# Moving weight loads of layer 0's experts behind its attention, and the order of the filling of layer 1

## The chip, the cores and the metric

The kernel runs on one core of a Trainium2 chip. The core has TensorE (PE, matrix products), VectorE (DVE), ScalarE (ACT), GpSimd (POOL) and SyncE (SP), which here only issues DMAs. Each engine runs its own program in order and waits on semaphores that others raise. The metric is the time of one execution on the device, in microseconds.

## What is computed

Two layers on 64 sequences of 64 positions and 256 channels, all in float32. Each layer is a cross attention and a mixture of experts, each with a residual:

```python
x = x + xattn0(layernorm(x), ctx)       # rotary, 8 heads of 8, projection
x = x + ffn0(layernorm(x))              # 64 experts, top 8, no capacity
x = x + xattn1(layernorm(x), ctx)       # 8 heads of 8
x = x + ffn1(layernorm(x))              # 64 experts, top 8, capacity 128 rows for each expert

def moe(x, router, gate, up, down):     # 4096 tokens
    topw, topi = top_k(softmax(x @ router), 8)
    topw = topw / topw.sum(-1)
    for each chosen expert e:  y += topw_e * (silu(x @ gate[e]) * (x @ up[e])) @ down[e]
```

An expert's weights are gate and up (128 x 384 floats, 192 KB) and down (96 x 256 floats, 96 KB).

## The kernel before

**Attention of a layer** is a software pipeline over 32 pairs of sequences. Step `s0` of it works on pair `s0 - LAG[stage]` at each stage: load 0, comb 1, front 2, stack 3, smax 4, attn 5, back 6, route 7, place 8, post 9. `steps` calls `body` on each engine for 41 steps, and most engines cut a step into 16 units `u`. Buffers are three deep (`NB`).

- *front*: the normalised rows `xn` are projected to q and k (`qk`, L1523). ScalarE, GpSimd and ScalarE again split them into three bf16 parts: `parts[0]` (L954), `rem` (GpSimd L779), `parts[1]` (ACT L963), and GpSimd's third part (L787).
- *stack*: SP writes the parts to DRAM (`q_stack_d`, `k_stack_d`, L621) and reads them back as stacked operands `q2`, `k2` (L645).
- *smax*: 16 score tiles `psS` (PE L1479), whose row maxima DVE takes (`mx`, L1086). The maxima of each half are turned (`mT0`), cut to bf16 (`mhi`, ACT) and a remainder (`mlo`, DVE `split_max`), and SP puts both into `q2` (L655).
- *attn*: the scores again, less the maxima, ScalarE's Exp into `prob` (L886), products with `v`.
- *route, place, post*: the router, the eight chosen experts, the row of each. In layer 0 GpSimd scatters every normalised row to its eight places in `xs_d` (L728).
- *comb*, layer 1 only: a step fetches the eight results of a pair with GpSimd's gathers `yg` (L741), four are scaled by ScalarE (`ys`, L893, `s_comb`), four are scaled and added by DVE (`add_row`, L1130, `s_sum`), which makes `x2` and its moments (`sums`). GpSimd's `roots` make the scale of the layer norm of it, ScalarE `xn`. SP stores `x2` to `x2_d` (L660); it is read again at attn. A gather waits until the buffer of the pair before has been used.

The first steps of layer 1, up to `FULL` = 6, have no full load for the units and an order of their own: `units_of_sum` and `units_of_products` place the sums and the products, and `sums` of pair 2 stand in step 4 after eight maxima.

**Experts of layer 0** are 320 tiles of 128 rows, sorted by expert. `slots` is a pipeline with one tile in each slot: gather by SP 4 slots behind, transposes (X) 8, gate and up products (GU) 9, transposition of the hidden tile (H) 10, down product (D) 11. ScalarE copies the transposed tile (`xgT`, L984), takes Silu (L989) and copies the result (`y_all`, L993). PE waits at every eighth slot for the weights of the next eight experts (`d_w`).

**Weights** go into `wt`, which shares SBUF with the attention's tiles and fills it from the top. Room for `EARLY` = 12 experts is left free by the attention, and ScalarE issues their loads in steps 9 to 14. The other 52 are issued by ScalarE, expert `s0 + 12` at the head of slot `s0`, so that nine loads stand before its first copy of a tile. Between the attention and the slots of a layer stands a barrier of all five engines; in layer 0 DVE makes a table of the tiles ahead of it, SP clears the end of the lists (`clear_end`) and reads the table, and GpSimd waits for its scatters.

What sets the order is the code itself: each engine's program is written out in the order in which it runs.

## Time and profile before

| | |
|---|---|
| median of 3 runs | 2065.82 us (2065.47 to 2069.38) |
| the profiled execution | 2065.41 us, of which the span of the trace is 2063.7 us |
| layer 0's attention | 0 to 605 us, scatters and table until the barrier opens at 647 |
| layer 0's experts | 647 to 1123 us |
| layer 1's attention | 1126 to 1798 us, its last routing until 1820 |
| layer 1's experts | 1820 to 2063 us |
| busy over the span | PE 81%, PE weight loads 55%, DVE 68%, ACT 61%, POOL 48% |

The slices of the page, each 51.6 us, show PE at 9 nearly everywhere but for two dips, around 625 us and around 1150 us, and the end. DMA-issuing instructions are not counted as busy, so an engine that issues loads looks idle in the profile and is not.

### The profile page before, as it was taken

The numbers are of one execution on the slowest core, as the hardware profiler recorded it, in microseconds if no ns is written. First come the engines' busy times: TensorE is split into PE (matmuls) and PEld (weight loads), VectorE is DVE, ScalarE is ACT, GpSimd is POOL, SyncE is SP. The second block draws the span as 40 slices with busy tenths as digits, with TensorE's granted clock in tenths as the row PEclk, the third lists the DMA queues.
The fourth block names the chain that finished last, engine by engine and source line by source line (L and its number), as shares of the span: only waits on it lengthen the run. The fifth ranks groups of instructions, "written<-read, shape, count | busy, mean of one in ns | idle before, by whom it ended". The sixth has DMA issues, their size and how long they took to land. (4 is left out here: it accounts for less than half of the span.)

```text
span 2063.7 us, 45000 instructions
## 1 busy us (share of the span) xinstructions
PE 1665.0 (81%) x12724; PEld 1130.1 (55%) x12879; DVE 1412.1 (68%) x4335; ACT 1264.0 (61%) x3300; POOL 985.5 (48%) x1114
## 2 busy tenths in 40 slices
PE   3999999999973999999997268888888888845651
PEld 1555555555543789888986134444444444444530
DVE  5888888888854455545434469999999999743330
ACT  1777677777761566666665258888888887621210
POOL 4367677777763000000001666666666663148883
PEclk9999999999995999999999589999999999969896
DMA  5678877777736966666665578898778876178856
GB/s 139 160 210 243 224 213 213 210 211 216 202 119 185 346 213 202 198 198 201 196 199 160 138 187 202 227 233 199 194 195 200 195 195 151 51 187 186 177 93 111
DMA packets 413088, 390.98 MB, mean 189 GB/s; under 512 B 46640, under 2 KB 385072, under 8 KB 412848
## 3 DMA queue, kind: packets, MB, share of 16 engines
q1 hardware_dynamic: 341888, 259.97, 47.3%
q0 software_dynamic: 37904, 90.22, 17.6%
q10 hardware_dynamic: 33056, 37.90, 6.2%
q8 instruction: 113, 1.85, 0.4%
q14 instruction: 127, 1.04, 0.2%
HBM read 233.74 MB, written 170.16 MB: 196 GB/s over the span
## 5 line engine op out<-in xcount | busy, mean ns | idle before, releaser
L1086 DVE TENSOR_REDUCE mx<-psS 128x2 f32<-128x512 f32 x1024 | 678.9, 674 | 112.3 <-PE psS L1479 72.5
L886 ACT ACTIVATE prob<-psE 128x512 f32<-128x512 f32 x1024 | 601.1, 595 | 227.6 <-PE psE L1492 211.6
L741 POOL DMA_INDIRECT yg<-y_d,row_all x256 | 249.7, 975 | 642.7 <-SPq L401 484.1
L1492 PE MATMUL psE<-q,k 128*128 128x256 bf16 x2048 | 395.2, 275 | 38.8 <-ACT prob L886 16.1
L1479 PE MATMUL psS<-k,q 128*128 128x512 bf16 x869 | 337.0, 390 | 32.8 <-DMA k<-k_stack_d 26.2
L1602 PE MATMUL psE<-wt,xgT 128*128 (+1 forms) x1536 | 325.8, 336 | 6.1 <-ACT xgT L984 5.6
L1431 DVE TENSOR_TENSOR hid<-sil,psE 128x96 f32<-128x96 f32 x384 | 97.6, 254 | 333.0 <-ACT sil L989 332.8
L728 POOL DMA_INDIRECT xs_d<-xr,row_all x256 | 252.6, 987 | 109.3 <-ACT prob L886 65.4
L1492 PEld LDWEIGHTS psE<-q,k 128*128 128x128 bf16 x2048 | 186.0, 98 | 194.3 <-ACT prob L886 70.6
L1508 PE MATMUL psO<-prob,v 128*32 128x256 f32 x4096 | 275.9, 387 | 8.5 <-ACT osb L866 8.5
L984 ACT COPY xgT<-psS 128x256 f32<-128x256 f32 x384 | 144.5, 376 | 197.4 <-PE psS L1596 137.5
L1602 PEld LDWEIGHTS psE<-wt,xgT 128*128 128x128 f32 x1536 | 247.9, 195 | 12.2 <-issue 10.8
L1596 PE MATMUL psS<-ident,xg 128*128 128x128 f32 x768 | 154.7, 284 | 100.5 <-DMA xg<-xn_d,idx 84.9
L1614 PE MATMUL psM<-wt,hT 96*128 (+1 forms) x768 | 233.1, 385 | 0.0
L1596 PEld LDWEIGHTS psS<-ident,xg 128*128 128x128 f32 x768 | 105.1, 144 | 159.7 <-DMA xg<-xn_d,idx 82.3
L1479 PEld LDWEIGHTS psS<-k,q 128*128 128x128 bf16 x1024 | 103.9, 102 | 153.2 <-issue 71.5
L993 ACT COPY y_all<-psM 128x256 f32<-128x256 f32 x320 | 119.2, 373 | 86.6 <-PE psM L1614 86.2
L1508 PEld LDWEIGHTS psO<-prob,v 128*32 128x32 f32 x4096 | 109.8, 109 | 104.1 <-issue 49.2
L989 ACT ACTIVATE sil<-psE 128x96 f32<-128x96 f32 x384 | 96.7, 252 | 88.2 <-PE psE L1602 87.6
L1614 PEld LDWEIGHTS psM<-wt,hT 96*128 96x128 f32 x768 | 118.1, 194 | 15.2 <-issue 0.4
L1523 PE MATMUL psM<-xn,proj_q 128*128 128x256 f32 x126 | 44.4, 436 | 74.0 <-ACT xn L930 37.5
L787 POOL TENSOR_TENSOR parts<-rem,parts 128x512 bf16<-128x512 f32 x64 | 74.9, 1171 | 50.3 <-ACT parts L963 49.4
(219 smaller groups left out, 2632.4 us busy)
## 6 DMA issues: line engine op xcount, KB each, us to landing
xg<-xs_d SPq DMA_DIRECT2D x320, 128.0 KB, 2.6
y_d<-y_all SPq DMA_DIRECT2D x320, 128.0 KB, 2.3
q<-q_stack_d SPq DMA_DIRECT2D x128, 256.0 KB
k<-k_stack_d SPq DMA_DIRECT2D x128, 256.0 KB
wt<-in_gu ACTq DMA_DIRECT2D x128, 192.0 KB, 3.7
q_stack_d<-parts SPq DMA_DIRECT2D x64, 192.0 KB
k_stack_d<-parts SPq DMA_DIRECT2D x64, 192.0 KB
wt<-in_dn ACTq DMA_DIRECT2D x128, 96.0 KB, 4.2
```

The lines of the kernel that those rows point to most:

```text
L728: g.indirect_dma_start(xs_d[:, :], bass.IndirectOffsetOnAxis(row_all[:, row(st.pair(stage) * K + k, 1)], 0), xr[b][:, 0:T], None).then_inc ...
L741: g.indirect_dma_start(yg[:, k, :], None, y0_d[:, :], bass.IndirectOffsetOnAxis(row_all[:, row(st.pair("load") * K + k, 1)], 0))\
L886: a.activation(prob[gr][:, u % 4, :], psE[ring][:, :], ACT.Exp, scale=SCALE).then_inc(s_exp, 1)
L984: a.copy(xgT[st.buf("X", 2)][:, :, :].rearrange("p c t -> p (c t)"), psS[st.buf("X", 2)][:, 0:2 * P]).then_inc(s_xgT, 1)
L993: a.copy(y[st.buf("D")], psM[st.buf("D", 2)][:, 0:T]).then_inc(s_y, 1)
L1086: v_.tensor_reduce(mx[b][:, bg // 4, :].rearrange("p (h r) -> p h r", h=2)[:, :, (bg % 4) * 2 + tt], psS[(UNITS * (st.s0 - LAG["smax"]) + ...
L1479: m_.matmul(psS[(UNITS * (st.s0 - LAG["smax"]) + u) % 3][:, :], q2[b][:, bg, tt * P:(tt + 1) * P], k2[b][:, bg, :], start=True, stop=True) ...
L1492: ins = m_.matmul(psE[ring][:, i * T:(i + 1) * T], k2[b][:, bg, hh * T + i * P:hh * T + (i + 1) * P], q2[b][:, bg, :], start=True, stop=True)
L1508: ins = m_.matmul(psO[32 * j:32 * j + 32, (q % 2) * T:(q % 2 + 1) * T], v[b][:, i, 4 * q + j, :], prob[gr][:, j, i * T:(i + 1) * T], start ...
L1596: ins = m_.transpose(psS[i][:, c * P:(c + 1) * P], xg[b][:, c * P:(c + 1) * P], ident[:, :])
L1602: ins = m_.matmul(psE[i][:, 0:2 * I], xgT[i][:, c, :], weights_of(st, "GU", table, P, 2 * I * c, 2 * I), start=(c == 0), stop=(c == 1))
L1614: m_.matmul(psM[i][:, 0:T], hT[i][:, :], weights_of(st, "D", table, I, 4 * I, T), start=True, stop=True).then_inc(s_yp, 1)
```

## The change

- The tiles `q2`, `k2` and `prob` are allocated last in the attention, so that, once they are no longer used, room for `FIRST` = 30 experts lies free at the top of SBUF.
- After the last step with a back stage in layer 0, SP waits for the last maxima, exponentials and products, and then issues experts 12 to 21, and after the last step experts 22 to 29 (`load_soon`). With nothing between them on SP, these are 18 experts in a row.
- ScalarE issues the other 34 in layer 0's slots, starting at slot 8, two in every three slots. In layer 1 nothing changes in this.
- ScalarE executes a Silu of one column ahead of the barrier in both layers, which loads the table for it.
- In layer 1 SP stores `x2` of a pair one step later, behind the reading of the stack and ahead of the maxima (before: behind the maxima and at once).
- In step 5 of layer 1 GpSimd does the first four gathers, then the remainder and the third part, then the other four.
- In step 4 of layer 1 DVE does `split_max` after eight maxima and ahead of pair 2's sums, not after eleven.

```diff
+SOON, LATER = 10, 8
+FIRST = EARLY + SOON + LATER
...
+        def load_soon(sp, first, n):
+            sp.wait_ge(s_max, UNITS * PAIRS)
+            sp.wait_ge(s_exp, UNITS * PAIRS)
+            sp.wait_ge(s_pv, 4 * PAIRS)
+            for e in range(first, first + n):
+                load_weights(sp, 0, e)
...
@@ block.sync, body
+                summed = Step(1, st.s0 - 1)
+                if L == 1 and summed.on("comb"):
+                    b, t = summed.buf("comb"), summed.pair("comb")
+                    hold(sp, s_x2, summed.n1("comb"))
+                    sp.dma_start(x2_d[row(t), :], x2[b][:, :]).then_inc(d_x2[b], 16)
                 if L == 0 and 0 <= st.s0 - CLEAR_AT < PAIRS:
...
-                if st.on("comb") and L == 1:
-                    b, t = st.buf("comb"), st.pair("comb")
-                    hold(sp, s_x2, st.n1("comb"))
-                    sp.dma_start(x2_d[row(t), :], x2[b][:, :]).then_inc(d_x2[b], 16)
                 if st.on("back"):
...
+                if L == 0 and st.s0 == LAG["back"] + PAIRS - 1:
+                    load_soon(sp, EARLY, SOON)
 
             for L in range(2):
                 steps(L, body)
+                if L == 0:
+                    load_soon(sp, EARLY + SOON, LATER)
...
@@ block.gpsimd, body, layer 1
-                    if st.s0 >= FULL - 1:
+                    if st.s0 >= FULL:
                         for k in range(K):
                             gather(st, k, PACE[L][k])
+                    elif st.s0 == FULL - 1:
+                        for k in range(4):
+                            gather(st, k, 0)
                     remainder()
                     third_part()
                     if st.s0 < FULL - 1:
                         for k in range(AHEAD_OF_ROOTS):
+                            gather(st, k, 0)
+                    elif st.s0 == FULL - 1:
+                        for k in range(4, K):
                             gather(st, k, 0)
...
@@ block.scalar
             def slot_body(st, table):
-                if st.s0 < E - EARLY:
-                    load_weights(act, st.L, st.s0 + EARLY)
+                for e in range((FIRST, EARLY)[st.L], E):
+                    if st.s0 == (FLAG["X"] + (e - FIRST) * 3 // 2, e - EARLY)[st.L]:
+                        load_weights(act, st.L, e)
...
             for L in range(2):
                 steps(L, body)
+                act.wait_ge((s_wk, s_wall)[L], PAIRS)
+                a.activation(ex[:, 0:1], ex[:, 0:1], ACT.Silu)
                 barrier(act, 2 + 2 * L)
...
@@ block.vector, body
+                filled = L == 1 and st.s0 == FULL - 2
...
-                    if u == 10 and st.on("smax"):
+                    if u == 10 and st.on("smax") and not filled:
                         split_max("smax", 0)
...
-                    if L == 1 and st.s0 < FULL - 2 - 1 and u == 15:
-                        sums(st, 0)
-                    if L == 1 and st.s0 == FULL - 2 and u == 7:
+                    if filled and u == 7:
+                        split_max("smax", 0)
                         sums(Step(1, FULL - 3), 0)
-                    if L == 1 and st.s0 == FULL - 2 and u == 15:
+                    if L == 1 and st.s0 < FULL - 1 and st.s0 != FULL - 3 and u == 15:
                         sums(st, 0)
```

ScalarE at the start of layer 0's slots. Before, behind the last router's exponential (`ex`), stand nine pairs of loads, here the end of them, and then the first tile:

```order
L522 DMA wt<-in_dn 96x256
L521 DMA wt<-in_gu 128x384
L522 DMA wt<-in_dn 96x256
L521 DMA wt<-in_gu 128x384
L522 DMA wt<-in_dn 96x256
L984 COPY xgT<-psS 128x256
L521 DMA wt<-in_gu 128x384
L522 DMA wt<-in_dn 96x256
L984 COPY xgT<-psS 128x256
L989 ACT_TABLE_LOAD
L989 ACTIVATE sil<-psE 128x96
```

The same place of the changed kernel, from the last exponential on:

```order
L999 ACTIVATE ex<-top,ntop 128x8
L1024 ACT_TABLE_LOAD
L1024 ACTIVATE ex<-ex 128x1
L526 DMA wt<-in_gu 128x384
L527 DMA wt<-in_dn 96x256
L1010 COPY xgT<-psS 128x256
L526 DMA wt<-in_gu 128x384
L527 DMA wt<-in_dn 96x256
L1010 COPY xgT<-psS 128x256
L1015 ACTIVATE sil<-psE 128x96
```

One pair of loads is left ahead of the first copy, and the table load stands ahead of the barrier.

SP in steps 3 and 4 of layer 1. Before, from the reading of pair 0's stack (`q_0`, `k_0`), the store of pair 2's x2 (`x_d<-x_2`) stands ahead of pair 1's stack:

```order
L645 DMA q_0<-q_stack_d 64x2048
L645 DMA k_0<-k_stack_d 64x8x256
L660 DMA x_d<-x_2 128x256
L570 DMA xin<-x_d 128x256
L621 DMA q_stack_d<-parts 128x3x256
L621 DMA q_stack_d<-parts 128x2x256
L621 DMA q_stack_d<-parts 128x256
```

The same place of the changed kernel:

```order
L659 DMA q_0<-q_stack_d 64x2048
L659 DMA k_0<-k_stack_d 64x8x256
L666 DMA x_d<-x_1 128x256
L584 DMA xin<-x_d 128x256
L635 DMA q_stack_d<-parts 128x3x256
L635 DMA q_stack_d<-parts 128x2x256
L635 DMA q_stack_d<-parts 128x256
```

In the place of pair 2's store now stands pair 1's, a step older; pair 2's stands behind the reading of pair 1's stack.

GpSimd in step 5 of layer 1. Before, with three gathers left over from step 4 in the 11:

```order
L759 TENSOR_TENSOR rstd<-below,rstd 128x2
L741 DMA yg<-y_d,row_all 128x256 x11
L779 TENSOR_TENSOR rem<-qk,parts 128x512
L787 TENSOR_TENSOR parts<-rem,parts 128x2x256
L754 TENSOR_SCALAR ve<-mv 128x2
```

The same place of the changed kernel:

```order
L778 TENSOR_TENSOR rstd<-below,rstd 128x2
L760 DMA yg<-y_d,row_all 128x256 x7
L798 TENSOR_TENSOR rem<-qk,parts 128x512
L806 TENSOR_TENSOR parts<-rem,parts 128x2x256
L760 DMA yg<-y_d,row_all 128x256 x4
L773 TENSOR_SCALAR ve<-mv 128x2
```

Four gathers moved from ahead of the remainder to behind the third part.

## Rows read from the trace of the kernel before

**Rows 1.** Timeline, first dip: start us, us, engine, line, operation, count, [idle before <-releaser].

```profile
610.49 0.33 SPq L664 DMA_DIRECT2D x_d<-x  x1
...
640.88 0.96 POOL L728 DMA_INDIRECT xs_d<-xr,row_all  x1 [0.30 <-issue]
...
647.37 0.33 ACTq L521 DMA_DIRECT2D wt<-in_gu  x1
...
650.84 1.17 PE L1596 MATMUL psS<-ident,xg 128*128 128x128 f32 x4 [14.74 <-DMA xg<-xs_d]
...
655.93 0.37 ACT L984 COPY xgT<-psS 128x256 f32<-128x256 f32 x1 [34.09 <-issue]
...
657.33 1.28 ACT L989 ACT_TABLE_LOAD   x1
```

**Rows 2.** Windows: busy us (instructions) by engine, PEclk, DMA share, GB/s; scatters.

```profile
605.00:642.00 37.00, 9.60 (x55) 5.52 (x45) 16.74 (x80) 3.82 (x10) 28.50 (x33) 0.61 0.29 101
```

**Rows 3.** Windows of layer 0's expert products, with and without weight loads.

```profile
662.00:727.00 65.00, 63.35 (x366) 52.26 (x365) 29.47 (x112) 35.96 (x122) 0.00 (x0) 1.00 1.07 344
737.00:1037.00 300.00, 300.00 (x1902) 269.67 (x1902) 149.85 (x572) 189.81 (x634) 0.00 (x0) 1.00 0.66 199
```

**Rows 4.** Timeline of ScalarE, one slot with a load.

```profile
668.17 0.37 ACT L993 COPY y_all<-psM 128x256 f32<-128x256 f32 x1 [0.18 <-PE psM L1614]
...
669.09 0.37 ACT L984 COPY xgT<-psS 128x256 f32<-128x256 f32 x1 [0.55 <-PE psE L1602]
...
669.67 0.37 ACT L993 COPY y_all<-psM 128x256 f32<-128x256 f32 x1
```

**Rows 5.** Timeline of SP's queue in the filling of layer 1.

```profile
1154.74 1.51 SPq L621 DMA_DIRECT2D q_stack_d<-parts  x3
...
1179.85 0.33 SPq L660 DMA_DIRECT2D x_d<-x  x1
...
1180.75 1.46 SPq L621 DMA_DIRECT2D q_stack_d<-parts  x3
```

**Rows 6.** Timeline of the other engines in the filling of layer 1.

```profile
1149.83 1.44 POOL L787 TENSOR_TENSOR parts<-rem,parts 128x512 bf16<-128x512 f32 x1 [0.73 <-ACT parts L963]
...
1164.86 1.15 POOL L787 TENSOR_TENSOR parts<-rem,parts 128x512 bf16<-128x512 f32 x1 [0.73 <-ACT parts L963]
...
1170.49 1.68 PE L1479 MATMUL psS<-k,q 128*128 128x512 bf16 x3 [9.40 <-DMA k<-k_stack_d]
...
1176.57 0.48 DVE L1130 SCALAR_TENSOR_TENSOR ys<-yg,w_all,xin 128x256 f32<-128x256 f32 x1
...
1177.02 0.26 ACT L873 CAST mhi<-psM 16x128 bf16<-16x128 f32 x1 [2.21 <-PE psM L1521]
...
1188.11 0.48 DVE L1130 SCALAR_TENSOR_TENSOR ys<-yg,w_all,xin 128x256 f32<-128x256 f32 x1 [2.56 <-DMA yg<-y_d,row_all]
...
1192.72 0.18 DVE L1168 BATCH_NORM_AGGREGATE mv<-stats 128x2 f32<-128x6 f32 x1
...
1194.89 0.69 DVE L1086 TENSOR_REDUCE mx<-psS 128x2 f32<-128x512 f32 x1 [1.99 <-PE psS L1479]
...
1195.88 0.24 POOL L754 TENSOR_SCALAR ve<-mv 128x2 f32<-128x2 f32 x1
...
1197.67 1.07 POOL L741 DMA_INDIRECT yg<-y_d,row_all  x1 [0.16 <-issue]
...
1206.53 0.95 POOL L741 DMA_INDIRECT yg<-y_d,row_all  x1 [5.26 <-ACT ys L893]
...
1217.81 0.62 ACT L963 CAST parts<-rem 128x512 bf16<-128x512 f32 x1 [6.76 <-POOL rem L779]
...
1234.86 1.16 POOL L779 TENSOR_TENSOR rem<-qk,parts 128x512 f32<-128x512 f32 x1
```

**Rows 7.** Timeline of ScalarE at the end of layer 1's attention.

```profile
1817.53 0.72 ACT L903 ACTIVATE hote<-hote,part 128x512 bf16<-128x512 bf16 x1 [3.40 <-DVE hote L1205]
...
1819.96 0.33 ACTq L521 DMA_DIRECT2D wt<-in_gu  x1
```

More of the change, by code:

```diff
@@ L284, in build @@
         parts = [ab(f"parts{b}", [P, 2, 3, T], BF16) for b in range(NB)]
-        q2 = [ab(f"q2_{b}", [P, 8, T], BF16) for b in range(NB)]
-        k2 = [ab(f"k2_{b}", [P, 8, 2 * T], BF16) for b in range(NB)]
         mx = [ab(f"mx{b}", [P, 2, 16]) for b in range(NB)]
@@ L290, in build @@
         v = [ab(f"v{b}", [P, 2, UNITS, 32]) for b in range(NB)]
-        prob = [ab(f"prob{g}", [P, 4, 512]) for g in range(3)]
         osb = ab("osb", [P, GROUPS, T])
@@ L321, in build @@
         zf = xr[0]
-        assert nc.sbuf_bytes_remaining >= 4 * EARLY * WIDTH
+        below_these = nc.sbuf_bytes_remaining
+        q2 = [ab(f"q2_{b}", [P, 8, T], BF16) for b in range(NB)]
+        k2 = [ab(f"k2_{b}", [P, 8, 2 * T], BF16) for b in range(NB)]
+        prob = [ab(f"prob{g}", [P, 4, 512]) for g in range(3)]
+        assert nc.sbuf_bytes_remaining >= 4 * EARLY * WIDTH and below_these >= 4 * FIRST * WIDTH
         att.close()
```

## The prediction

> **What bounds the kernel now.** I read the slices of the page first: layer 0's attention, a dip near 625 us, the expert products of layer 0 up to 1123 us, a second dip, layer 1's attention, its products. The change touches the two dips and the first 50 slots of the products of layer 0, so I opened the timeline at both dips and the windows by stage.
>
> First dip [rows 1]. The last attention output is stored at 610.49, but GpSimd goes on scattering rows, one each 1.26 us (0.96 busy, 0.30 idle), until 641.8. The barrier opens at 647.4. GpSimd bounds this stretch; the DMA engines are 0.29 busy [rows 2]. Then TensorE has the first tile transposed from 650.84, but ScalarE copies it only at 655.93: it was issuing the weights of nine experts, 18 DMAs. Five microseconds of a waiting TensorE are ScalarE's queue.
>
> Layer 0's products. Nine multiplies are one tile. While weights are loaded, 366 of them take 65 us, so 40.7 tiles at 1.60 us; afterwards 1902 take 300 us, 211.3 tiles at 1.42 us [rows 3]. ScalarE's loop shows why that can be: with a load a slot lasts 1.50 us, 0.55 us of it a gap for the issue [rows 4]. But the DMA share is 1.07 there, 0.66 later [rows 3], so two limits coincide.
>
> Second dip [rows 5, 6]. Here the filling of layer 1's pipeline waits on one queue, SP's. The third bf16 part of pair 0 is ready at 1151.27 (1149.83 + 1.44), its stack goes out at 1154.74. Pair 1's is ready at 1166.02 and goes out at 1180.75, right behind the store of pair 2's x2 at 1179.85, which SP had to wait for. TensorE's first scores, after 9.40 us idle, and step 5's wait for those stacks. Later ScalarE is idle 6.76 us for GpSimd's remainder of pair 3, which stands behind eight gathers.
>
> **The change, part by part.**
>
> 1. Weights of experts 12 to 29 on SP from 610.9. SP issues 36 DMAs; at ScalarE's rate (18 in the 8.56 us from 647.37 to 655.93, 0.48 each) they take 17 us, until 628. Moved behind them on SP: the clearing of the end of the lists and the reading of the table, for which SP waits until DVE has it; the barrier needs GpSimd's scatters to land anyway, 19 us after 628, so the 17 us on SP cost nothing. What of DMA capacity? In the loading window a tile without loads would take 0.66 x 1.42 = 0.94 us of all engines; it takes 1.07 x 1.60 = 1.71, so an expert costs 0.77 us. A scatter costs 0.29 x 37 / 27 = 0.40 us (33 instructions of GpSimd, six of them roots) [rows 2, 3]. From 611 to 642: 18 x 0.77 + 25 x 0.40 = 23.9 us in 31, and in the 17 us of issue 19.4 against 18.2 at a share of 1.07: a backlog of about 1 us, gone by 632. I take zero for the barrier; between a gain, which nothing on this path could give, and a delay, if scatters run at half rate for those 17 us, 14 x 1.26 = up to 17 us. Near zero is the row's own value, since the sum fits.
>
> The Trainium skill (DMA: Bandwidth & Descriptors, Issuing engines are not separate DMA queues) says that DMAs of all engines run on the same 16 engines and interleave, so that another issuer saves issue time only. By it the 18 experts are no cheaper on SP than on ScalarE and the sum for the barrier stands or falls with the capacity above; ScalarE's issue time is what is saved, as items 2 and 3 have it. No row before shows scatters beside SP loads.
>
> 2. ScalarE's head start. The 16 DMAs of slots 0 to 7 are gone; slot 8 issues one pair before the tile arrives. The copy can follow the transposes by 0.65 us: 651.5 instead of 655.93, **4.4 us**; between 3.9 and, if the tile lands earlier without the weights beside it, 5.4.
>
> 3. The pace. 34 experts are left, at two per three slots, up to slot 57. Two slots of 1.50 and one of 0.95 (1.50 less the gap of 0.55) are 1.32 us of ScalarE per slot, under TensorE's 1.42. The DMA demand becomes 0.66 + 34 x 0.77 / 71 = 1.03, just under 1.07. The excess was 65 - 40.7 x 1.42 = 7.2 us. If each load kept its price, 34/40.7 of it would remain: a gain of 1.2. If none did, 7.2. I take **5.8**, nearer the second because both limits are then undershot, one barely.
>
> 4. The Silu table. Its load of 1.28 us [rows 1] leaves layer 0's first slots, where TensorE ran on beside it: 0.2 us, between 0 and 0.5. In layer 1 it stands between the copy for the lists (ends 1818.25) and the barrier, past which ScalarE issues at 1819.96 [rows 7]: 1.28 and a one-column Silu just fit. Zero, between -0.4 and +0.3.
>
> The Trainium skill (ScalarE: Activation LUTs, What ACT_TABLE_LOAD costs) puts a drain of about 1.38 us behind each such load. Estimated by that page, layer 1's barrier would come about 1 us later and the total would be 1 us higher; the row before has 1.28 and shows no drain, which speaks against it here.
>
> 5. The fill. I move each event by what released it. Pair 0's stack: 1154.74 becomes 1151.3, so -3.4, and the first scores (1170.49) come at 1167.1. In step 4 VectorE now waits for the split of the maxima ahead of the sums: the bf16 maxima end at 1177.28 and the subtraction at 1177.55, against sums that started at 1176.57, +1.0. So pair 2's sums, the last gathers of pair 3 that wait for them, and pair 3's sums move by -2.4. VectorE ended those at 1192.90 and then waited until 1194.89 for the stack; now the stack is there first (its store moves by up to 14.7; the context load behind it on SP waits for pair 0's V product, still 10 us ahead of before) and step 5 starts at 1190.5, -4.4. Three score tiles are ready by then, which saves perhaps 0.6 more: pair 5's first gather moves from 1206.53 to 1201.5. Then the remainder stands behind four gathers, not eight: 1201.5 + 4 x 1.26 = 1206.5, done 1207.6, where ScalarE had it at 1217.81: -10.2. That is not kept. GpSimd now is the chain: the remainder and third part to 1209.6, four gathers to 1214.7, the roots (1.8, from 1195.88 to 1197.67), eight gathers to 1226.6, and the remainder of step 6 starts there instead of 1234.86: **8.2 us**. By then GpSimd has caught up (8 x 1.26 + 3.1 + 1.8 = 15 us of work in a step of 18). Below, if the sums or the products ahead of the gathers refuse to move with the stack, it is 3; above, if GpSimd's gathers in step 6 overlap better than drawn, 10.5.
>
> 6. In all later steps of layer 1 SP stores x2 one step later, between the stack's loads and the maxima. It waits for nothing there, and VectorE carries these steps. Zero; between -3 and +5 over 27 steps, since a DMA ahead of the maxima could cost 0.2 a step.
>
> Sum: 4.4 + 5.8 + 0.2 + 0 + 8.2 = 18.6. The profiled execution took 2065.4, of which the span is 2063.7; that is 0.4 below the median 2065.8. So 2046.8 on its scale, **2047** on the median's.
>
> **The rivals.**
>
> A. The fill gives 3 only, since VectorE's sums of pair 3 wait for gathers, which wait for sums (the 2.0 us behind 1192.90 is all the stack itself held). For it: at 1188.11 pair 3's sums start after 2.56 us of waiting for a gather; against: GpSimd's gathers demonstrably stand ahead of the remainder. 2047 + 5.2 = 2052.
>
> B. In the products the DMA engines, not ScalarE, are the limit, and at 1.03 they still are: 1.2 instead of 5.8, 2052. Against: demand falls by a third.
>
> C. The weights slow the scatters. Each later scatter waits for its turn: half rate for half of the 17 us gives 8.5 back, 2056.
>
> D. Slower than before: the same place as C, but GpSimd's issue itself stalls while SP's descriptors fill the engines, and the whole row of about 25 scatters stretches. It decides from 18.6 / 25 = 0.74 us more per scatter (1.26 to 2.0); at 1.0 more the time is 2072. Against: the demand of that stretch fits, as item 1 has it.
>
> E. It doesn't do what it says: the barrier moves by as much as the products gain and the fill only shifts waits; within 4 us of before.
>
> F. Parts 3 and 5 at their upper ends: 2042.
>
> The Trainium skill (DMA: Bandwidth & Descriptors, Queues, rings and completion order) says that each DMA engine takes turns between the queues that have work. By this rule the scatters' queue keeps its turn and C and D would not occur; no row of before tests it, so they keep their chances.
>
> **How the numbers follow.** Forecast 0.50, A 0.16, B 0.12, C 0.07, D 0.04, E 0.03, F 0.08. The forecast's own spread is 2043 to 2051. The upper bounds of items 2, 3 and 5 together give 2042, the lower ones 2058 (3.9 + 1.2 + 3 = 8.1). A range of 2040 to 2058 leaves out D, E, and half of F: about 0.15 with the tails. A measurement of this kernel tells 0.2%, 4 us, from no change. Faster by more: all but D, E, 0.93; within 0.2%: 0.03; slower: 0.04.
>
> **What would show it.** Right: SP issues 36 weight DMAs between 611 and 629 and the barrier stays at 647.4; first copy of a tile at 651.5; tiles at 1.42 to 1.48 us from the start; counted from layer 1's first gather, pair 0's stack 3.4 us, pair 1's 11 to 15, step 5's first maximum 4 and the remainder of step 6 8 us earlier than before. Wrong: a barrier past 650; tiles still at 1.55 with ScalarE's gaps gone (B); step 5 moved but the remainder of step 6 not (A); steps of layer 1 longer than before by more than 0.2 us.

## The result, and the profile after

Timed in turn with the kernel before, the changed kernel took 2050.23 us in the median (2047.69 to 2055.02, 4 runs) against 2066.34: a ratio of 0.9922, 95% interval 0.9906 to 0.9939. Timed again in another series it had 2051.67 us, 0.9938 (0.9926 to 0.9951). It is 13 to 16 us faster where 18.8 were forecast; 2047 was 3 to 5 us too low, within the range of 2040 to 2058.

The profiled execution of after took 2055.02 us, its span is 2053.3, 10.4 below before. Cut at events that both traces have (the last scatter; the first transposed tile's copy; the first, 71st and last of ScalarE's 320 copies of a tile's product; layer 1's first gather and its first transposed tile's copy), that span divides like this, in us:

| stretch | before | after | gain | forecast |
|---|---|---|---|---|
| start to the last scatter | 640.88 | 641.82 | -0.9 | 0 |
| last scatter to the first transposed tile's copy | 15.05 | 10.72 | 4.3 | 4.4 |
| from there to the first product's copy | 6.1 | 6.1 | 0 | 0.2 |
| 70 tiles, while weights are loaded | 107.6 | 107.6 | 0.0 | 5.8 |
| the other 249 tiles | 353.1 | 354.6 | -1.5 | 0 |
| last product's copy to layer 1's first gather | 3.2 | 2.5 | 0.7 | 0 |
| layer 1's attention, to its first tile's copy | 702.6 | 694.6 | 8.0 | 8.2 |
| layer 1's experts | 235.2 | 235.2 | 0.0 | 0 |

Two terms of the sum are there, within 0.2 us each, and one is missing in this pair of traces. Two rows vary too much to be read: the 249 tiles without loads took 352.5 to 355.4 us in the kernels below that leave them alone, and the last scatter stands at 637.9 to 643.8 us in the other traces of kernels that took 2049 to 2059 us (641.5 in fill_only, which has no loads on SyncE there). This profiled execution is also the slowest of its four, so its 10.4 us is less than the 16.1 us between the medians; which stretch was quicker in the others no trace shows. The first dip first, in the timeline of after (start us, us, engine, line, operation, count, [idle before <- releaser]); it answers to [rows 1]:

```profile
612.10 0.33 SPq L679 DMA_DIRECT2D x_d<-x  x1
612.54 0.38 SPq L526 DMA_DIRECT2D wt<-in_gu  x1
...
622.80 1.28 ACT L1024 ACT_TABLE_LOAD   x1
...
641.82 0.96 POOL L747 DMA_INDIRECT xs_d<-xr,row_all  x1 [0.30 <-issue]
...
648.33 0.33 ACTq L526 DMA_DIRECT2D wt<-in_gu  x1
...
652.54 0.37 ACT L1010 COPY xgT<-psS 128x256 f32<-128x256 f32 x1 [27.92 <-PE psS L1624]
```

SyncE issues weights from 612.54, and GpSimd's last scatter still is 0.96 us with 0.30 us of idle time ahead. The barrier opens 6.5 us behind that scatter, as before. ScalarE has one pair of loads left ahead of its first copy, at 652.54, which waits for the transposes and no longer for ScalarE's own issues.

The windows (stretch, then busy us and instructions of PE, PE weight loads, DVE, ACT, POOL; PEclk, DMA share, GB/s), against [rows 2] and [rows 3]:

```profile
605.00:642.00 37.00, 11.06 (x59) 6.76 (x59) 17.31 (x84) 5.72 (x14) 28.43 (x36) 0.61 0.77 244
662.00:727.00 65.00, 62.50 (x367) 51.94 (x366) 29.46 (x111) 36.00 (x123) 0.00 (x0) 1.00 0.94 288
```

In the first dip the DMA engines went from a share of 0.29 to 0.77 and GpSimd did as much as before. In the second line is the surprise: with a third fewer loads (27 experts in these 65 us, before 40) and a DMA share of 0.94 instead of 1.07, 65 us hold 367 multiplies, before 366.

The filling of layer 1, against [rows 5] and [rows 6]; layer 1's first gather is at 1123.49 here, at 1125.94 before:

```profile
1148.76 1.45 SPq L635 DMA_DIRECT2D q_stack_d<-parts  x3
...
1157.72 0.62 SPq L666 DMA_DIRECT2D x_d<-x  x1
...
1163.49 1.43 SPq L635 DMA_DIRECT2D q_stack_d<-parts  x3
```

```profile
1164.24 2.49 DVE L1114 TENSOR_REDUCE mx<-psS 128x2 f32<-128x512 f32 x4 [12.19 <-remote]
...
1182.26 0.48 DVE L1158 SCALAR_TENSOR_TENSOR ys<-yg,w_all,xin 128x256 f32<-128x256 f32 x1 [2.54 <-DMA yg<-y_d,row_all]
...
1186.98 1.86 DVE L1114 TENSOR_REDUCE mx<-psS 128x2 f32<-128x512 f32 x3
...
1203.39 1.17 POOL L798 TENSOR_TENSOR rem<-qk,parts 128x512 f32<-128x512 f32 x1
...
1223.97 1.16 POOL L798 TENSOR_TENSOR rem<-qk,parts 128x512 f32<-128x512 f32 x1
```

Counted from the first gather, pair 0's stack goes out 25.27 us later (28.80 before), pair 1's 40.00 (54.81), since no store stands ahead of it that waits. Pair 3's sums start at 58.77 (62.17), still after 2.54 us of waiting for a gather. Step 5's first maximum starts right behind them at 63.49 (68.95), without the wait for the stack, and the remainder of step 6, 1223.97 - 1123.49 = 100.48, was at 108.92.

### The profile page after: what moved, and what is told of

Read it like the earlier page. It is cut to its first block and busy times, and to the rows that moved or that the text cites. A ratio compares the mean times of both kernels' runs of the same rounds, so it can differ in the third digit from the quotient of the medians.

```text
span 2053.3 us, 45004 instructions
## 1 busy us (share of the span) xinstructions
PE 1665.0 (81%) x12724; PEld 1127.2 (55%) x12879; DVE 1414.6 (69%) x4335; ACT 1265.1 (62%) x3302; POOL 983.7 (48%) x1114
## 5 line engine op out<-in xcount | busy, mean ns | idle before, releaser
L760 POOL DMA_INDIRECT yg<-y_d,row_all x256 | 248.7, 971 | 632.2 <-SPq L406 480.7
L1507 PE MATMUL psS<-k,q 128*128 128x512 bf16 x869 | 336.5, 389 | 22.4 <-DMA k<-k_stack_d 12.8
L1624 PEld LDWEIGHTS psS<-ident,xg 128*128 128x128 f32 x768 | 103.7, 143 | 165.2 <-DMA xg<-xn_d,idx 90.7
L806 POOL TENSOR_TENSOR parts<-rem,parts 128x512 bf16<-128x512 f32 x64 | 74.8, 1169 | 50.4 <-ACT parts L988 49.5
```

The source lines that it names most:

```text
L760: g.indirect_dma_start(yg[:, k, :], None, y0_d[:, :], bass.IndirectOffsetOnAxis(row_all[:, row(st.pair("load") * K + k, 1)], 0))\
L1507: m_.matmul(psS[(UNITS * (st.s0 - LAG["smax"]) + u) % 3][:, :], q2[b][:, bg, tt * P:(tt + 1) * P], k2[b][:, bg, :], start=True, stop=True) ...
L1624: ins = m_.transpose(psS[i][:, c * P:(c + 1) * P], xg[b][:, c * P:(c + 1) * P], ident[:, :])
```

## Where the missing term went

For each kernel I took the starts of ScalarE's copies of tile products (y_all from psM). The time from one start to the next is called a slot below. An undisturbed tile takes 1.415 us. The last columns count the slow slots and give what they have over 1.415 us each. The first 54 tiles, in us:

| kernel | first, 55th copy at | 54 tiles | over 54 x 1.415 | slots of 1.45 to 1.9: number, excess | slots over 1.9 |
|---|---|---|---|---|---|
| before | 662.00, 746.87 | 84.9 | 8.5 | 27, 6.6 | 3, 1.8 |
| after | 658.71, 743.64 | 84.9 | 8.5 | 25, 5.9 | 3, 2.5 |
| after, again | 659.73, 744.38 | 84.6 | 8.2 | 30, 6.9 | 1, 1.3 |
| fill_only | 662.47, 748.62 | 86.1 | 9.7 | 28, 6.6 | 4, 3.0 |
| weights_only | 653.77, 737.80 | 84.0 | 7.6 | 29, 6.9 | 1, 0.6 |
| loads_on_sp | 654.04, 751.49 | 97.5 | 21.0 | 16, 3.1 | 15, 17.9 |
| split_loads | 680.89, 765.61 | 84.7 | 8.3 | 22, 5.1 | 3, 3.2 |
| loads_on_pool | 687.43, 772.65 | 85.2 | 8.8 | 13, 2.8 | 4, 5.9 |
| late_even | 690.93, 774.37 | 83.4 | 7.0 | 33, 7.0 | 0, 0 |
| late_pairs | 686.09, 771.04 | 84.9 | 8.5 | 29, 5.9 | 3, 2.5 |
| in_slot | 693.37, 773.51 | 80.1 | 3.7 | 9, 1.6 | 6, 3.6 |
| in_slot_even | 692.70, 773.66 | 81.0 | 4.5 | 8, 1.7 | 3, 3.0 |
| in_slot_lead5 | 658.17, 737.88 | 79.7 | 3.3 | 9, 1.5 | 3, 2.7 |
| sp_order_only | 692.10, 776.05 | 84.0 | 7.5 | 27, 6.5 | 1, 0.9 |

Some slots under 1.4 us follow long ones, so the excess of the groups need not add up to the total. The six from split_loads to in_slot_even, and sp_order_only, were timed where the kernel before itself took 2177 or 2187 us, so their ratios are within 0.3 to 0.4% only; I use their traces for the pace (an undisturbed tile takes 1.415 us there too) and their ratios for little.

One trace of each kernel is also little for the difference between before and after. Two traces have the loads of before (before, fill_only) and took 107.6 and 109.3 us for 70 tiles; four have those of after (after, its repetition, weights_only, sp_order_only) and took 107.6, 107.6, 106.8 and 106.7. The change of the pace gained 1.3 us by these means, between 0.0 and 2.6 by single pairs.

## The experiments

**after, once more.** The changed kernel without an edit.

> The changed kernel once more, as the measure for its variants. From its first runs 2047.7 to 2055.0, so about 2050. In its profile so far, with the first filling gather of layer 1 as zero: the remainder of step 6 at 100.5 us (108.9 before). From the opening of layer 0's barrier to that gather 475.2 us (478.6 before), though 10.4 less was forecast. If a tile in the stretch with weight loads takes 1.53 us here too, the pace (not the fill) is the term that failed; if it takes 1.45, the first profile was a disturbed one.

2051.67 us, ratio 0.9938 (0.9926 to 0.9951). The stages repeat: 10.47 us from the last scatter to the first copy, 107.6 us for 70 tiles, pair 1's stack 40.06 us and step 6's remainder 100.54 us behind the first gather.

**fill_only.** ScalarE's loads as before, none on SyncE; the new order of the filling and the early Silu stay.

```
-                for e in range((FIRST, EARLY)[st.L], E):
-                    if st.s0 == (FLAG["X"] + (e - FIRST) * 3 // 2, e - EARLY)[st.L]:
-                        load_weights(act, st.L, e)
+                if st.s0 < E - EARLY:
+                    load_weights(act, st.L, st.s0 + EARLY)
...
-                    load_soon(sp, EARLY, SOON)
...
-                    load_soon(sp, EARLY + SOON, LATER)
```

> The changed kernel with ScalarE's weight loads of layer 0 as before (52 in the slots from slot 0, none on SP); the new order of the filling and the Silu ahead of the barriers stay. If the fill is worth the 8.4 us of the profile: 2066 - 8.5 = 2057.5, and what is left to the weights is 7 to 8. If the fill's gain is given back later in layer 1 (rival A): 2062 or more. The remainder of step 6 should stand 100.5 us after the first gather either way.

2055.85 us, ratio 0.9958 (0.9944 to 0.9971): 8.7 us gained (6.0 to 11.6). The last scatter starts at 641.54 and the first copy at 656.99, 15.45 us later, as before the change. Step 6's remainder is 99.1 us behind the first gather.

**weights_only.** The filling in its old order on SyncE, GpSimd and VectorE; the weights moved.

```
-                summed = Step(1, st.s0 - 1)
-                if L == 1 and summed.on("comb"):
...
+                if st.on("comb") and L == 1:
...
-                    if st.s0 >= FULL:
+                    if st.s0 >= FULL - 1:
...
-                    if u == 10 and st.on("smax") and not filled:
+                    if u == 10 and st.on("smax"):
```

> The changed kernel with the filling of layer 1 in the old order on SP, GpSimd and DVE. Theory: head start of ScalarE 4.4 us, pace 1.5, so 2066 - 6 = 2060. If the two halves of the change add up, this gain and that of the filling alone make 16 us together. If the forecast's 5.8 for the pace were there and only hidden in one profile: 2055.5.

2058.01 us, ratio 0.9968 (0.9956 to 0.9979): 6.6 us gained (4.3 to 9.1). Items 2 to 4 of the sum promised 10.4 together; item 2 alone is 4.4. The first copy came 10.63 us behind the last scatter, and 54 tiles took 84.0 us. The two halves gained 8.7 and 6.6 us, 15.3 together, and the whole 12.8 in the same series (10.1 to 15.3), so they add up within the noise. Both halves of the change therefore pay, and it is the half with the weights that pays too little.

**loads_on_sp.** SyncE issues the 34 pairs in the same slots.

```
+            for e in range(FIRST, E):
+                if st.s0 == FLAG["X"] + (e - FIRST) * 3 // 2:
+                    load_weights(sp, 0, e)
             if st.on("gather"):
```

> The changed kernel, but SP instead of ScalarE issues the 34 expert loads in layer 0's slots, in the same slots: the same DMAs, none of them on ScalarE. Theory 1 (the issue of a pair of loads, 0.8 us, stands in ScalarE's loop between the copy of a result and the copy of a tile, and two slots in a row with it outrun the slack, so TensorE waits): tiles at 1.42 to 1.44 us, ScalarE's gaps of 0.55 gone, 5 to 6 us faster than the changed kernel, 2045. Theory 2 (rival B: the DMA engines at a share of 0.95 delay the tiles' gathers): still 1.53 us for a tile, 2050. A third way: the loads delay SP's own gathers and stores, and it is slower, above 2052.

2058.84 us, ratio 0.9969 (0.9957 to 0.9981): slower than after. Neither theory said so, but the third way of the expectation did: the loads delay SyncE's own gathers and stores. 54 tiles took 97.5 us. SyncE's queue in the timeline of this kernel:

```profile
671.65 0.43 SPq L566 DMA_DIRECT2D y_d<-y_all  x1
672.13 0.43 SPq L526 DMA_DIRECT2D wt<-in_gu  x1
672.60 0.48 SPq L527 DMA_DIRECT2D wt<-in_dn  x1
673.27 0.34 SPq L561 DMA_DIRECT2D xg<-xs_d  x1
673.65 0.43 SPq L566 DMA_DIRECT2D y_d<-y_all  x1
674.27 0.34 SPq L561 DMA_DIRECT2D xg<-xs_d  x1
674.65 0.47 SPq L566 DMA_DIRECT2D y_d<-y_all  x1
```

A slot with a load costs SyncE 2.0 us (671.65 to 673.65), one without 1.0. Two of the first and one of the second are 5.0 us where TensorE has three tiles in 4.25. SyncE's issues became the bound, and TensorE waited 10.5 us in twelve waits for tiles. But ScalarE's regular slots of 1.70 us were gone; in the first seven tiles six took 1.41 or 1.42. The Trainium skill (DMA: Bandwidth & Descriptors, Issuing engines are not separate DMA queues) says that several issuers save only sequencer time, "usually small relative to the DMA itself". Here this sequencer time is what decides: the same transfers from the other queue cost 12.6 us.

**split_loads.** The two transfers of an expert in different slots: 68 single issues, the n-th in slot 8 + 3n/4, still ahead of the transposed tile's copy.

```
+                if st.L == 0:
+                    for n in range(2 * (E - FIRST)):
+                        if st.s0 == FLAG["X"] + n * 3 // 4:
+                            half_of_weights(act, FIRST + n // 2, n % 2)
```

> Same 68 transfers for the 34 experts in the same stretch, on ScalarE's queue, but the two transfers of an expert are no longer issued together: 68 single issues are spread over the slots 8 to 58 (n-th issue at slot 8 + 3n/4), so a slot holds one or two of them. The first 54 tiles of layer 0 took 84.9 us after the change where 54 undisturbed tiles take 76.5 (1.417 each), and 17 of them, the second of two loaded slots in a row, took 1.70 instead of 1.42. Theory 1 (the cost is ScalarE's own issue time of 0.33 + 0.45 us between two copies, which the slack of one slot takes in but that of two in a row does not): the 1.70 slots vanish or shrink, up to 17 x 0.28 = 4.8 us less, 54 tiles in 80 to 81 us, about 2047 us. Theory 2 (the DMA engines, busy to 0.91 there, set the pace): bytes and density are the same, so 54 tiles still take about 85 us, about 2051.5 us.

0.9947 (0.9911 to 0.9984), 54 tiles in 84.7 us: nothing gained. The pattern of 1.42, 1.42, 1.70 us stayed. So theory 1 in the form "two in a row overrun the slack" gains no support. Every third slot still has two issues, and its trace tells more: the transposed tile's copy follows the product's copy by 0.44 us where one issue stands between them and by 0.92 where two do, and where its pattern is plain, only the slot behind the two is slow. A delay of 0.17 us is hidden, one of 0.65 is not.

**loads_on_pool.** GpSimd issues the 34 pairs, held back by the count of transposed tiles.

```
+                if L == 0:
+                    for e in range(FIRST, E):
+                        at = Slot(0, FLAG["X"] + (e - FIRST) * 3 // 2)
+                        pool.wait_ge(s_xp, at.n("X"))
+                        load_weights(pool, 0, e, d_wp)
```

> GpSimd, which does nothing in the expert stage of layer 0, issues the 34 pairs of weight loads, held back slot by slot by the count of transposed tiles, so at the slots of the change; ScalarE issues none in layer 0. Theory 1 (ScalarE's issue time): no 1.70 us slots are left, 54 tiles in about 80 us (the rare stalls of 0.4 to 1.3 us may stay), about 2047 us. Theory 2 (DMA engines): the same bytes in the same stretch, 54 tiles still in about 85 us, about 2051.5 us. Against both: GpSimd's transfers could take their engines' time in another way than the ones ScalarE issues, and delay the tiles' reads as the loads on SyncE did (PE waited 9.2 us for the tiles there): then 90 us or more for 54 tiles and about 2058 us.

0.9921 (0.9892 to 0.9949), 54 tiles in 85.2 us. Both mechanisms show at once. With ScalarE free, the first four slots take 1.42, 1.41, 1.42 and 1.42 us and only 13 lie between 1.45 and 1.9. But four slots took 2.4 to 3.3 us. One of them, in the timeline of TensorE:

```profile
728.78 0.44 PE L1633 MATMUL psS<-ident,xg 128*128 128x128 f32 x2 [1.02 <-DMA xg<-xs_d]
```

The tile's read had not landed. Together these waits gave back what ScalarE had gained.

**late_even and late_pairs.** Loads in slots 8, 10, ... 74, and in the second kernel at the same rate but two in a row and two free. TensorE waits for the later groups of weights later, which is right for this input's routing only.

```
+                due = {8: 0, 16: 1, 24: 2, 32: 3, 40: 4, 56: 5, 72: 6, 88: 7} if layer == 0 else \
...
-                    if st.s0 == (FLAG["X"] + (e - FIRST) * 3 // 2, e - EARLY)[st.L]:
+                    if st.s0 == (FLAG["X"] + 2 * (e - FIRST), e - EARLY)[st.L]:
```

> The loads of the 34 experts stand in every second slot (8, 10, ... 74) on ScalarE; TensorE's waits for the later groups of weights move to slots 40, 56, 72 and 88, which suffices for the routing of this input but not for every one. No two loaded slots are neighbours. Theory 1 (two loaded slots in a row overrun ScalarE's slack): no 1.70 us slots, 4.8 us less than the change, first 54 tiles in 80 to 81 us, about 2047 us. Theory 2 (DMA engines): the load rate falls from 0.67 to 0.5 experts per slot, which frees the engines as well: 54 tiles in 78 to 82 us, again about 2047; told apart by the next kernel.

> The same rate as the kernel with every second slot (34 experts over 68 slots, the same moved waits), but two loaded slots in a row and then two free ones. Theory 1: each of the 17 pairs still costs 0.28 us, as in the change itself: a pattern of 1.42, 1.70, 1.42, 1.42 us, 17 x 0.28 = 4.8 us in all, about 2051.5 us, and 4.8 us slower than every second slot. Theory 2 (the DMA engines' load): as every second slot, about 2047 us, since the bytes per stretch of four slots are the same.

Ratios 0.9957 (0.9923 to 0.9990) and 0.9948 (0.9917 to 0.9980). 70 tiles took 107.5 and 110.8 us. Both forecasts for late_even failed: its loads are neighbours nowhere, and it has more slow slots than any other kernel, 33, of 0.2 us each, and no slot over 1.9. With 27 loads beside these 54 tiles that is 0.26 us for every load. Two loads in a row cost 0.28 together where after shows its plain pattern (1.42, 1.42, 1.70). What costs is the first load behind a free slot; in a run, as before, every second one. In late_pairs the 14 pairs beside the 54 tiles had 5.9 us in slow slots, 0.42 each and not the 0.28 of theory 1, and the kernel was 1.5 us slower than late_even there, not 4.8: why two free slots make a pair dearer than one is open.

The timeline of ScalarE in after shows why:

```profile
679.51 0.37 ACT L1019 COPY y_all<-psM 128x256 f32<-128x256 f32 x1 [0.23 <-PE psM L1642]
679.78 0.38 ACT L1010 COPY xgT<-psS 128x256 f32<-128x256 f32 x1
...
680.93 0.37 ACT L1019 COPY y_all<-psM 128x256 f32<-128x256 f32 x1 [0.29 <-PE psM L1642]
680.93 0.33 ACTq L526 DMA_DIRECT2D wt<-in_gu  x1
681.30 0.45 ACTq L527 DMA_DIRECT2D wt<-in_dn  x1
681.85 0.37 ACT L1010 COPY xgT<-psS 128x256 f32<-128x256 f32 x1 [0.55 <-PE psE L1630]
...
682.34 0.37 ACT L1019 COPY y_all<-psM 128x256 f32<-128x256 f32 x1
682.35 0.33 ACTq L526 DMA_DIRECT2D wt<-in_gu  x1
682.72 0.46 ACTq L527 DMA_DIRECT2D wt<-in_dn  x1
683.27 0.37 ACT L1010 COPY xgT<-psS 128x256 f32<-128x256 f32 x1 [0.56 <-issue]
```

and that of TensorE:

```profile
680.73 0.38 PE L1624 MATMUL psS<-ident,xg 128*128 128x128 f32 x2
680.95 0.81 PE L1630 MATMUL psE<-wt,xgT 128*128 x4
...
682.14 0.42 PE L1624 MATMUL psS<-ident,xg 128*128 128x128 f32 x2
682.56 0.91 PE L1630 MATMUL psE<-wt,xgT 128*128 x4
...
683.85 0.38 PE L1624 MATMUL psS<-ident,xg 128*128 128x128 f32 x2
684.07 0.82 PE L1630 MATMUL psE<-wt,xgT 128*128 x4
```

Without a load the transposed tile is copied 0.27 us behind the product's copy, with one 0.92 us. TensorE's gate and up product of that tile then starts 0.42 us behind the transposes ahead of it, not 0.22, and the loop falls back by 0.28. The second load delays its copy by as much, but TensorE is now 0.28 later itself and finds the tile ready (0.22 again). A free slot lets ScalarE catch up, and the next load pays anew. ScalarE was not short of time on average: in the row at 680.93 it has waited 0.29 us for TensorE. It did the wrong thing first. That the place of the issue is the cause is tested next.

**in_slot.** The same loads in the same slots; the two issues stand behind the transposed tile's copy and behind the Silu, where ScalarE waits anyway.

```
                     a.copy(xgT[st.buf("X", 2)][:, :, :].rearrange("p c t -> p (c t)"),
                            psS[st.buf("X", 2)][:, 0:2 * P]).then_inc(s_xgT, 1)
+                for e in range(FIRST, E):
+                    if st.L == 0 and st.s0 == FLAG["X"] + (e - FIRST) * 3 // 2:
+                        half_of_weights(act, e, 1)
...
+                for e in range(FIRST, E):
+                    if st.L == 0 and st.s0 == FLAG["X"] + (e - FIRST) * 3 // 2:
+                        half_of_weights(act, e, 0)
```

> The same loads in the same slots as the change, but the two issues of an expert no longer stand ahead of the transposed tile's copy: the one of the down projection (0.45 us) stands behind that copy and the one of gate and up (0.33 us) behind the Silu, where ScalarE waits 0.5 and 0.3 us in every slot anyway. What the traces so far show: after the change and with split loads every group of loads costs one slot 0.28 us (1.70 instead of 1.42), with loads every second slot each costs 0.25, and with GpSimd or SyncE issuing these 1.70s are gone, but reads of tiles land late instead (up to 1.9 us a time, 5.9 us in all with GpSimd). Theory 1b (the copy of the transposed tile is delayed by the 0.8 us of issue ahead of it, TensorE waits for it): the 1.70s vanish, the first 54 tiles take some 79 to 81 us against 84.9, and layer 0's experts end 4 to 5 us earlier. Theory 3 (two limits one behind the other: at 0.67 experts per slot a full pace asks for 256 + 0.67 x 288 = 449 KB in 1.415 us, 317 GB/s, of the some 340 GB/s that the engines moved at most in these 80 us): the 1.70s vanish but late reads of tiles take their place, 54 tiles still in 83 to 86 us.

54 tiles in 80.1 us, 4.8 less, as theory 1b had it, and theory 3's 83 to 86 is out. The four traces with the loads of after have 84.0 to 84.9, and the two kernels that follow, with issues in the same places, 81.0 and 79.7. From the last scatter to layer 1's first gather 475.4 us pass; in after 481.7, in its repetition 480.7, in weights_only and sp_order_only 478.8 and 480.5. The ratio, 0.9935 (0.9904 to 0.9966), can't tell this from after.

```profile
717.21 0.37 ACT L1032 COPY y_all<-psM 128x256 f32<-128x256 f32 x1 [0.23 <-PE psM L1655]
717.48 0.38 ACT L1017 COPY xgT<-psS 128x256 f32<-128x256 f32 x1
...
718.63 0.37 ACT L1032 COPY y_all<-psM 128x256 f32<-128x256 f32 x1 [0.29 <-PE psM L1655]
718.85 0.32 ACTq L532 DMA_DIRECT2D wt<-in_dn  x1
718.90 0.38 ACT L1017 COPY xgT<-psS 128x256 f32<-128x256 f32 x1
...
719.51 0.35 ACTq L534 DMA_DIRECT2D wt<-in_gu  x1
720.04 0.37 ACT L1032 COPY y_all<-psM 128x256 f32<-128x256 f32 x1 [0.29 <-PE psM L1655]
720.27 1.19 ACTq L532 DMA_DIRECT2D wt<-in_dn  x1
```

In this timeline the transposed tile's copy follows at 0.27 us with or without a load. The last row is what remains: an issue of 1.19 us. The six slots over 1.9 start 14.6, 26.7, 29.8, 43.3, 46.4 and 58.3 us behind the first product's copy, each within 3 us of such a long issue on ScalarE (12.5, 26.9, 44.2, 59.2).

**in_slot_even.** The places of in_slot at the rate of late_even.

> The same places inside a slot, and loads in every second slot only (8 to 74; TensorE's waits for the later groups moved as in late_even, which suffices for this input's routing alone). A full pace then asks for 400 KB in 1.415 us, 283 GB/s. Both theories: with both limits removed the first 54 tiles take 77 to 79 us (76.5 undisturbed), 6 to 8 us less than after the change, the sum of an item that gained nothing there. If it still takes 83 us or more, neither the issue on ScalarE nor the rate of the transfers is the cause.

0.9942 (0.9909 to 0.9974), 54 tiles in 81.0 us, not 77 to 79. The regular slow slots are gone here too (8 left), and the lower rate brings nothing on top of in_slot. So the rate of the transfers is not what the last 3 to 4 us hang on. What was measured lies under the 83 at which both causes would have fallen.

**in_slot_lead5.** in_slot, with tiles read five slots ahead.

```
-        FLAG = dict(idx=0, gather=4, X=8, GU=9, H=10, D=11)
+        FLAG = dict(idx=0, gather=3, X=8, GU=9, H=10, D=11)
```

> The change with the two issues moved inside their slot (behind the transposed tile's copy and behind the Silu, as in in_slot), and the read of a tile issued five slots ahead of its use, not four, in both layers. With in_slot the 1.70 us slots were gone, 54 tiles took 80.1 us against 84.9 (76.5 undisturbed), and of the 3.7 us left 3.6 stood in six slots of 1.9 us and more. If those are reads that land late (theory 3: four slots are 5.7 us, the reads took 4.0 us in the median), one slot more takes in most of them: 54 tiles in 77.5 to 79.5 us, layer 0's experts 5 to 7 us shorter than after the change, and a ratio to the kernel before of about 0.990 to 0.992 where the change alone had 0.994. If they are long issues on ScalarE and SyncE (single ones of 0.7 to 1.8 us were seen), the lead changes nothing: 80 us again, about 0.992. Layer 1's experts wait for reads issued by GpSimd, which is busy itself; there nothing or up to 2 us.

2049.25 us against 2063.35, ratio 0.9916 (0.9896 to 0.9936), the lowest of all ratios but not separable from after's 0.9922 and 0.9938. 54 tiles took 79.7 us: no better than in_slot, so late reads are not what is left there, and the long issues are the candidate that stands. The remaining tiles got worse: 249 in 357.6 us, 352.7 with in_slot, with 27 slots between 1.45 and 1.9 us against 6. Why five slots of lead cost that is open.

**sp_order_only.** Of the new order in the filling, SyncE's alone.

> The change without the new order on GpSimd and VectorE in the fill of layer 1: of the three edits there only SyncE's (the store of the finished sum one step later, behind the stack writes) stays. The whole fill took 8.4 us less from the first gather of layer 1 to the sixth step's routing. Theory A (SyncE's queue was the limit there: its store waited for the sum while the stack writes stood behind it): pair 0's and 1's stack is written as early as after the change (25.3 and 40.0 us from the first gather), and 4 to 6 of the 8.4 us stay. Theory B (GpSimd's gathers are): at most 2 us stay, the rest needs GpSimd's and VectorE's order. The expert stage of layer 0 is the change's.

0.9954 (0.9920 to 0.9989). Its first gather is at 1156.05:

```profile
1181.36 1.45 SPq L635 DMA_DIRECT2D q_stack_d<-parts  x3
...
1196.10 1.43 SPq L635 DMA_DIRECT2D q_stack_d<-parts  x3
```

```profile
1239.27 1.16 POOL L798 TENSOR_TENSOR rem<-qk,parts 128x512 f32<-128x512 f32 x1
1259.44 1.17 POOL L798 TENSOR_TENSOR rem<-qk,parts 128x512 f32<-128x512 f32 x1
```

The stacks go out at 25.31 and 40.05 us, the whole shift. The remainder of step 5 starts at 83.2 us (90.7 before, 79.9 after), that of step 6 at 103.4 (108.9 and 100.5). So some 5.5 of the 8.4 us are SyncE's store, theory A. GpSimd's and VectorE's order, not tried apart, have the rest, some 3.

## Why the prediction was right or wrong

**Item 1, right.** Zero for the barrier. SyncE was done with its issues at 631, not 628, and the scatters kept their 1.26 us, though from 612.5 to 631.2, while SyncE issued, the DMA share was 1.02 (0.77 over the whole dip). C and D would have needed them to stretch.

**Item 2, right.** 4.4 forecast, 4.3 measured, and fill_only, which puts all the weight loads back on ScalarE, has 15.45 us there again.

**Item 3, wrong: 5.8 forecast, 0.0 measured in the pair of before and after, 1.3 in the mean of the six traces.** The step that failed is "Two slots of 1.50 and one of 0.95 (1.50 less the gap of 0.55) are 1.32 us of ScalarE per slot, under TensorE's 1.42". It compared a mean of one engine with the pace of another, and looked neither at where in the slot the issue stands nor at who waits for the copy behind it. With the issues moved behind that copy, in_slot gained the 4.8 us. The lower end of the item, 1.2 us if each load kept its price, is about what came: the price belonged to every second load of a run, and to every pair now, and the first 54 tiles have 27 slow slots with 40 loads beside them before and 25 with 31 after. Rival B gave the right total for this item with the wrong cause. The DMA engines were not the limit at a share of 0.94, for in_slot moved the same bytes 4.8 us faster. Whether in before, at 1.07, they would have set about the same pace by themselves was not tried, so that the two limits of [rows 3] coincided there is neither shown nor refuted.

**Item 4, right in kind.** In layer 0 the load at 622.80 hides and the 6.1 us from the first transposed tile's copy to the first product's copy did not change, so the 0.2 us don't show. In layer 1, the load of 1.28 us stands at 1807.56:

```profile
1806.82 0.72 ACT L928 ACTIVATE hote<-hote,part 128x512 bf16<-128x512 bf16 x1 [3.40 <-DVE hote L1234]
1807.56 1.28 ACT L1024 ACT_TABLE_LOAD   x1
1808.85 0.20 ACT L1024 ACTIVATE ex<-ex 128x1 f32<-128x1 f32 x1
1809.25 0.34 ACTq L526 DMA_DIRECT2D wt<-in_gu  x1
```

From the end of the copy for the lists, 1807.54, to the first issue behind the barrier are 1.71 us, and 1.71 before (1818.25 to 1819.96). The Trainium skill (ScalarE: Activation LUTs, What ACT_TABLE_LOAD costs) adds a drain of about 1.38 us to each such load. By that page the barrier would have come about 1 us later, an estimate. Here the load starts 0.02 us behind the copy and the Silu 0.01 us behind the load, and the measurement decides against the drain.

**Item 5, right.** 8.2 forecast, 8.4 measured at the remainder of step 6, and each event on the way within 1.1 us: pair 0's stack -3.5 (-3.4), pair 1's -14.8 (11 to 15), step 5's first maximum -5.5 (-4.4). Rival A's chain is there: pair 3's sums wait 2.54 us for a gather (2.56 before), and they, not the stack, now stand ahead of step 5's first maximum. But the chain itself moved by 3.4 us (2.4 forecast), the 2.0 us behind it are gone, and four gathers fewer stand ahead of step 5's remainder, so the fill did not stop at A's 3 us.

**Item 6, right.** Zero; from the remainder of step 6 to the first transposed tile's copy of layer 1 the two traces differ by 8.4 - 8.0 = 0.4 us over all the steps.

With item 3 at 0, the sum is 4.4 + 0.2 + 8.2 = 12.8 us, which would have said 2053; with 1.3 it is 14.1, 2052. The gain of the second series is 12.8 us (10.1 to 15.3); the first series has 3 us more, which no trace explains. So 2047 came as near as it did in part by luck: a third of its sum was hardly there, and what the first series had besides made up for some of it.

## What to carry to other kernels

In this kernel an issue of a transfer in a compute engine's loop cost what it delayed, not what it added to the mean: look which instruction stands right behind it, and put it where that engine waits for another. To move a limit away from an engine's queue, count the issues of the receiving queue first; SyncE had 1.0 us of them per slot of 1.4, and no room for another 1.0 in two slots of three. And a chain of releases followed event by event, as in the filling, is worth more than a comparison of loads.

## What the hardware showed that I had not expected

About every 15 to 18 us one issue takes 0.7 to 2 us instead of 0.33 to 0.45, and where ScalarE and SyncE both issue, it often hits both at the same time and ends together. In the timeline of after's repetition:

```profile
719.43 1.81 ACTq L527 DMA_DIRECT2D wt<-in_dn  x1
719.97 1.27 SPq L558 DMA_DIRECT2D xg<-xs_d  x1
721.34 0.37 ACT L1010 COPY xgT<-psS 128x256 f32<-128x256 f32 x1 [1.91 <-PE psS L1624]
...
722.04 0.91 PE L1630 MATMUL psE<-wt,xgT 128*128 x4 [1.39 <-ACT xgT L1010]
```

Both end at 721.24, and TensorE waits 1.39 us. On SyncE of in_slot such issues start 12.5, 27.1, 44.2, 59.2, 74.8 and 90.1 us behind the first product's copy, the last two when no weights are loaded any more. With loads on GpSimd they are on SyncE alone. When an issue on ScalarE is hit, the copy behind it is late too, and this cost TensorE up to 1.4 us a time. What causes them is not known.
